# Order of transposes, logits, clearing and gate transfers at the entries of two expert blocks

## What is computed

```
x = conv attention (L0), then channel attention (L1)
t = tokens of x
t = t + L2_attn(layernorm(t))        # attention over the 8 images, per position
t = t + L2_ffn(layernorm(t))         # 8 experts, hidden 512, gelu, top 2 of softmax gates
t = t + L3_attn(layernorm(t))        # attention over the 256 positions, per image
t = t + L3_ffn(layernorm(t))         # 8 experts, hidden 256, silu(x w1) * (x w3), top 2, renormalised
```

```
logits = x @ gate_w + gate_b ; w = softmax(logits) ; keep the two largest, others 0
h = gelu(x @ w1[e] + b1[e])          # L3: silu(x @ w1[e]) * (x @ w3[e])
out = sum over e of gate[e] * (h @ w2[e] + b2[e])
```

## Time and profile before

| | us |
|---|---|
| median of 3 runs | 662.9 |
| lowest, highest | 662.83, 667.42 |
| profiled execution, its own time | 668.46 |
| its span in the profile | 666.7 |
| busy PE, DVE, ACT, POOL | 612.5, 535.1, 400.6, 146.0 |
| first expert block (layer 0) | starts at 152.6 |
| second expert block (layer 1) | starts at 505.2, to the end |

### The profile page before, as it was taken

The page is one execution under the profiler, slowest core; times in us unless marked ns, Lnnn a source line. Parts: engine busy times, 40 slices in busy tenths (PEclk is TensorE's granted clock), DMA queues, the critical chain, the costliest instruction groups (busy, mean ns, idle before and its releaser), DMA issues. The chain is left out here.

```text
span 666.7 us, 10013 instructions
## 1 busy us (share of the span) xinstructions
PE 612.5 (92%) x3186; PEld 483.1 (72%) x3186; DVE 535.1 (80%) x1153; ACT 400.6 (60%) x792; POOL 146.0 (22%) x117
## 2 busy tenths in 40 slices
PE   9998959997989999999997889999868889999996
PEld 5785458695768888887886777777746678888784
DVE  2736679967678778878788799999996699999986
ACT  4613221002958888888884799999873455555552
POOL 1193366645211101111011121111103011111200
PEclk9697587997889999999999555555556999999998
DMA  5000000002212220222000000000001242222200
GB/s 181 1 0 1 0 1 1 0 1 65 89 73 95 97 75 21 95 95 63 1 1 0 1 2 0 0 0 0 1 2 48 73 163 74 99 79 92 72 33 31
DMA packets 9699, 28.78 MB, mean 43 GB/s; under 512 B 960, under 2 KB 3264, under 8 KB 9536
## 3 DMA queue, kind: packets, MB, share of 16 engines
q1 hardware_dynamic: 9664, 28.34, 12.3%
HBM read 27.15 MB, written 1.18 MB: 43 GB/s over the span
## 5 line engine op out<-in xcount | busy, mean ns | idle before, releaser
L1327 DVE TENSOR_TENSOR hL<-hraw,hH 128x1024 fp32r<-128x1024 f32 (+1 forms) x128 | 131.4, 1053 | 35.2 <-ACT hH L1063 34.5
L1143 PE MATMUL ps<-xH,wH 128*128 128x512 f32 x256 | 103.5, 404 | 4.2 <-DVE hraw L1257 3.6
L1067 ACT ACTIVATE hraw<-ps,bias 128x512 f32<-128x512 f32 x128 | 86.8, 687 | 31.1 <-PE ps L1145 26.7
L1144 PE MATMUL ps<-xL,wH 128*128 128x512 f32 x256 | 102.7, 401 | 0.0
L1145 PE MATMUL ps<-xH,wL 128*128 128x512 f32 x256 | 102.6, 401 | 0.0
L996 POOL TENSOR_TENSOR wL<-wraw,wH 128x1024 fp32r<-128x1024 f32 (+1 forms) x16 | 35.6, 2227 | 236.1 <-DVE wH L1194 236.1
L1155 PE MATMUL ps<-hH,wH 128*128 128x512 f32 x192 | 77.2, 402 | 7.9 <-DVE hL L1327 7.9
L1157 PE MATMUL ps<-hH,wL 128*128 128x512 f32 x192 | 76.5, 398 | 0.0
L1156 PE MATMUL ps<-hL,wH 128*128 128x512 f32 x192 | 76.4, 398 | 0.0
L1063 ACT ACTIVATE hH<-hraw 128x1024 fp32r<-128x1024 f32 x64 | 67.5, 1055 | 1.0
L1072 ACT ACTIVATE hraw<-ps 128x512 f32<-128x512 f32 x64 | 38.3, 600 | 49.4 <-PE ps L1145 47.8
(11 more groups left out here) (247 smaller groups left out, 1197.3 us busy)
## 6 DMA issues: line engine op xcount, KB each, us to landing
G<-gates_scratch SPq DMA_DIRECT2D x32, 512.0 KB, 4.7
wraw<-in_ex SPq DMA_DIRECT2D x8, 514.5 KB, 5.7
wraw<-in_ex SPq DMA_DIRECT2D x8, 384.0 KB, 5.0
w<-in_pack SPq DMA_DIRECT2D x1, 1420.5 KB, 7.8
xs<-in_x SPq DMA_DIRECT2D x4, 256.0 KB, 4.6
out<-acc SPq DMA_DIRECT2D x4, 256.0 KB, 2.1
w<-in_pack SPq DMA_DIRECT2D x1, 501.0 KB, 3.7
gates_scratch<-gT SPq DMA_DIRECT2D x4, 32.0 KB
```

Of the source, the lines that this page charges most:

```text
L1067: act.activation(hraw[:, k % 2, h, :], ps[:, h, :], ACT.Gelu, bias=bias[:, place(k, last)[0], h:h + 1]).then_inc(z["act"], 1)
L1143: pe.matmul(o, wH[:, p, at:at + P], xa, start=True, stop=False)
L1144: pe.matmul(o, wH[:, p, at:at + P], xb, start=False, stop=False)
L1327: dve.tensor_tensor(hL[:, k % 2, g * half:(g + 1) * half, :], src, hi.bitcast(F32), ALU.subtract).then_inc(z["hl"], 1)
```

## The change

Numbered by place:

1. In `block2`, POOL clears acc behind the last normalisation scale of that block, once DVE has normalised the first half. In the entry of layer 0 only cmp is cleared, and not before DVE has normalised the second half.
2. In the entry of layer 0 the second half of the tokens is transposed with a signal after four columns and after eight, ACT copies it in two parts, and the logits follow each part. The filler before these logits is gone (the two fillers behind the first half's logits stay).
3. In layer 1 the logits of pair 0 come before the transposes of pair 1, the others behind the transposes of pair 3, and the filler is gone.
4. The residual transposes of pair 2 move from the end of the attention block into the entry of layer 1, those of pair 3 behind the transposed gates, into bank 6. The transposed gates wait for three copies of acc instead of four, and DVE's wait for acc moves in front of its first addition.
5. The first gate transfer is cut: the first 512 tokens of expert 0 are a transfer of their own with a semaphore of its own (`g0`), on which DVE's first gating waits. The second gating waits for the rest of the first half.

```diff
@@ block2, gpsimd
             ln_pool(pool, 1, 0)
+            pool.wait_ge(ln["nrm"], S + 1)
+            pool.memset(acc[:], 0.0).then_inc(s_rot, 1)
@@ experts, sync
                     for a_half in range(2):
                         c = slice(a_half * T // 2, (a_half + 1) * T // 2)
-                        sp.dma_start(G[:, p, c], gd[layer][bass.ds(e, 1), c].to_broadcast([P, T // 2])).then_inc(zw[p][1 + a_half], 16)
+                        if isinstance(j, int) and e == 0 and a_half == 0:
+                            sp.dma_start(G[:, 0, 0:CH], gd[layer][0:1, 0:CH].to_broadcast([P, CH])).then_inc(z["g0"], 16)
+                            c = slice(CH, T // 2)
+                        sp.dma_start(G[:, p, c], gd[layer][bass.ds(e, 1), c].to_broadcast([P, c.stop - c.start])).then_inc(zw[p][1 + a_half], 16)
@@ experts, gpsimd
                 if layer == 0:
                     ln_pool(pool, nn, 1)
-                chp.done(pool.memset(cmp[:], 0.0))
-                if layer == 0:
-                    pool.memset(acc[:], 0.0).then_inc(s_rot, 1)
+                    pool.wait_ge(ln["nrm"], S * nn + 2)
+                    pool.memset(cmp[:], 0.0).then_inc(s_rot, 1)
                 else:
+                    chp.done(pool.memset(cmp[:], 0.0))
                     pair_pool(pool, 3, c4)
@@ experts, scalar
                 if layer == 0:
-                    act.wait_ge(gs["ltp"], 2)
-                    act.activation(lnT[:, 1, :], flat(ps[:, 2:4, :]), ACT.Copy).then_inc(gs["lt"], 1)
+                    for g in range(2):
+                        act.wait_ge(gs["ltp"], 2 + g)
+                        act.activation(lnT[:, 1, g * CH:(g + 1) * CH], ps[:, 2 + g, :], ACT.Copy).then_inc(gs["lt"], 1)
                 else:
                     for c in range(NCH):
-                        if c == 2:
-                            tokens_out(act, 3, 7)
+                        if c == 1:
+                            tokens_out(act, 2, 7)
...
                         act.activation(gT[:], ps[:, 7, 0:P], ACT.Copy).then_inc(gs["gT"], 1)
+                        if layer == 1:
+                            tokens_out(act, 3, 6)
@@ experts, tensor
                     for s in range(S):
-                        pe.wait_ge(gs["lt"], s + 1)
-                        if s == 1:
-                            keep_busy(pe, 5, 1)
                         for b in range(B):
+                            if b % 4 == 0:
+                                pe.wait_ge(gs["lt"], s + 1 + s * (b // 4))
                             x = logits(s * B + b, lnT[:, s, b * P:(b + 1) * P])
                         if s == 0:
                             keep_busy(pe, 5, 2)
-                            ln_transposes(pe, nn, gs["ltp"], 1)
+                            ln_transposes(pe, nn, gs["ltp"], 1, 0, 4)
...
-                        pe.wait_ge(c4["acc"], NCH)
+                        pe.wait_ge(c4["acc"], 3)
...
                         gates_transposed()
+                        if layer == 1:
+                            tokens_transposed(pe, 3, 6)
@@ experts, vector
-                    dve.wait_ge(gs["lt"], s + 1)
+                    dve.wait_ge(gs["lt"], 1 + 2 * s)
...
-                    if c % 2 == 0:
+                    if isinstance(j, int) and item == 0:
+                        dve.wait_ge(z["g0"], 16)
+                    elif c % 2 == 0 or (isinstance(j, int) and item == 1):
                         dve.wait_ge(zw[p][1 + c // 2], 16 * (j + 1))
...
+                    if isinstance(j, int) and item == 0:
+                        dve.wait_ge(s_rot if layer == 0 else c4["acc"], 2 if layer == 0 else NCH)
...
-                dve.wait_ge(s_rot if layer == 0 else c4["acc"], 2 if layer == 0 else NCH)
@@ block4, scalar
-            for c in range(3):
+            for c in range(2):
                 tokens_out(act, c, SB + c)
@@ block4, tensor
-            tokens_transposed(pe, 2, SB + 2)
```

More of the change, by code:

```diff
@@ L941, in rounds @@
                     yield E // 2 - 1, k, True
-            z = {n: sem(f"ex{layer}_" + n) for n in "split wH hp act hm hH hl yp yg acc".split()}
+            z = {n: sem(f"ex{layer}_" + n) for n in "split wH hp act hm hH hl yp yg acc g0".split()}
             zw = [[sem(f"ex{layer}_{n}{p}") for n in ("w", "ga", "gb")] for p in range(2)]
-            fin = {n: sem(f"fin{layer}_" + n) for n in "tp done st".split()}
+            fin = {n: sem(f"fin{layer}_" + n) for n in ("tp done" if layer == 0 else "st").split()}
             nn = 1 + layer
@@ L1101, in _, with pair_logits @@
                             keep_busy(pe, 5, 2)
-                            ln_transposes(pe, nn, gs["ltp"], 1)
+                            ln_transposes(pe, nn, gs["ltp"], 1, 0, 4)
                 else:
-                    pair_transposes(pe, 0, c4)
-                    pair_transposes(pe, 1, c4)
-                    tokens_transposed(pe, 3, 7)
-                    keep_busy(pe, 4, 1)
-                    pair_transposes(pe, 2, c4)
-                    pair_transposes(pe, 3, c4)
-                    for c in range(NCH):
+                    def pair_logits(c):
                         pe.wait_ge(c4["lt"], c + 1)
@@ L1113, in _ @@
                             x = logits(i % 2 * B + 2 * c + i // 2, pair_columns(c)[:, i * P:(i + 1) * P])
+                        return x
+                    pair_transposes(pe, 0, c4)
+                    tokens_transposed(pe, 2, 7)
+                    pair_logits(0)
+                    for c in range(1, NCH):
+                        pair_transposes(pe, c, c4)
+                    for c in range(1, NCH):
+                        x = pair_logits(c)
                 x.then_inc(gs["lgp"], 1)
@@ L1241, in _ @@
                 if layer == 0:
-                    dve.wait_ge(s_rot, 2)
+                    dve.wait_ge(s_rot, 3)
                 for i in range(E):
```

## The result

| | before | changed |
|---|---|---|
| median of 20 runs each, side by side | 667.12 (661.27 to 670.88) | 660.77 (658.61 to 666.19) |
| ratio, 95% interval | | 0.9927 [0.9907, 0.9948] |
| own time and span of the profiled execution | 668.46, 666.7 | 661.98, 660.2 |

The change makes the kernel faster by 0.73%. The predicted 656.7 us is 4.1 us too low, and the median lies 0.27 us above the top of the range. The move itself was forecast nearly right: 656.7/662.9 is 0.9906, just under the interval above. Five executions of over 820 us, two of the kernel before and three of edited ones, are left out of every median here.

What follows compares the result with a forecast made beforehand. PE was taken as bound, busy in both expert blocks behind their entries, so microseconds won at entries stay won. 2.6+1.0+1.03-0.2+1.0 = 5.4, plus 0.8 for the clock, 6.2 off 662.9: 656.7 us, range 652.5 to 660.5.

Steps and rivals of the forecast that it cites:

- Against the median I take 5.4+0.8 = 6.2, so 656.7 us: Whole kernel: summed gains of 5.4 us plus 0.8 for half clock, taken from the three-run median of 662.9 us.
- The chain of entry one: Entry of the first expert block: DVE's gate chain starts at 163.2 instead of 165.86, a gain of 2.6 us.
- The clearing's move: Entry one: acc's clearing (1.9 us) costs nothing in the attention block; the eight xc end 1.73 us earlier.
- The chunk: Gate transfer in both entries: first gating waits for 256 KB less, a gain of 1.0 us each, between 0 and 2.6.
- The half clock behind the gate wait: Entry one, behind PE's wait for hL: no clock fall, 1.7 us in the profiled execution, 0.8 counted against the median.
- The block's end: End of the attention block: without the third token transpose and ACT's copy, DVE's add is last, a gain of 1.03 us.
- Entry two, -0.2: Second expert block's entry: new order with logits at half clock loses 0.2 us, between a 0.6 loss and 2.6 gain.
- The token pair behind the gates: Entry two, token pair 3 transposed while PE waits for hL: hidden, costing 0, at most 0.3 us.
- A: Rival, chance 0.20: entry two's logits at full clock (2.4 us more), entry one's cast early (0.6): 653.7 us.
- B: Rival, chance 0.17: the gate chunk lands no earlier; both 1.0 gains and the clock's 0.8 go: 659.5 us.
- C: Rival, chance 0.08: POOL holds entry one, wL is late, the chain gains 1.5 instead of 2.6 us: 657.8 us.
- D: Rival, chance 0.04: without fillers PE stays at half clock through each block's first 36 matmuls; slower, 665.7 us.

## Why the prediction was wrong

**The step that failed** is "Against the median I take 5.4+0.8 = 6.2, so 656.7 us". Its 6.2 is near what was measured: medians of 667.12 and 660.77 are 6.35 apart, the means of those runs 4.95 (665.97 and 661.02), the interval of the ratio allows 3.5 to 6.2, and the two repeats give 6.8 and 7.4 between medians. What failed is the time that it is taken from, the median of three runs: two of three lay near 662.9, where this kernel's median is 667. From 667.1 the same sum gives 660.9. The profiled execution, 5.6 us over that median, was the warning; I set 1.7 us of it down to a dip that the others might lack and left the rest open. The remark that below 1% a measurement can't tell this change from none was wrong too: 0.73% stands clear of it, with 20 runs of each.

**The chain of entry one, 2.6.** lg moved by 2.4 us and the ups by 2.0, with the forecast's mechanism (the cast ends with wL) and another cause for wL's time: the weights' landing, not the clearing. What passed through was G's issue, 24.77 to 22.08, so 2.7; on the means of three profiles it is 3.2. It follows the ups, not lg: the gates' transposition stands behind 24 ups on PE, and they take 7.1 to 8.5 us by the clock. That "PE's clock in the first 24 matmuls matters less" was wrong, and the right size of the term came out by luck: the ups moved less than expected and ran through faster (8.4 to 7.7).

**The clearing's move.** That its 1.9 us "cost nothing" held. Its benefit, which the chain counts with 1.73 us on the xc, was nothing where the weights landed late and up to 0.8 us for wL where they landed early: the sum had no term for the landing.

**The chunk, 1.0 per entry.** On the means of three profiles, 4.25 to 3.26 us in entry one and 4.30 to 3.26 in entry two: 1.0 each, as worked out from the rate. The estimate of 0.6 that followed from the Trainium skill ("DMA: Bandwidth & Descriptors", section "Anatomy of one DMA — SWDGE (gpsimd) path") is too little on this queue. That all landing rows here are longer than its rule gives is not so: out's 256 KB took 2.1 us, less than the 2.6 that one would estimate by that rule.

**The half clock behind the gate wait, 1.7.** In entry one no profile with the change has it, but of three of before only the first did (177.6 us from G's issue to the last gating against 175.5 and 175.9), so counting half of it was somewhat too much. In entry two, for which the sum has no such term, the changed kernel's second profile and those of nine edited kernels fell to 1.2 GHz for 3.4 us behind waits of 1.9 to 2.7 us, while five others, with waits of 1.85 to 2.1, did not. The length of the last wait alone doesn't decide it. The kernel before kept its clock in entry two behind a longer wait than any of these:

```profile
535.30 0.50 PE L1143 MATMUL ps<-xH,wH 128*128 128x512 f32 x1 [2.90 <-DVE hraw L1257]
```

In its third profile it fell at 528.4 (0.50 in the window from 528.5 to 531.5), behind a wait of only 1.21 us that ended at 527.4, where the prediction expects no fall. In the changed kernel the stretch from the first gating to the end takes 132.8 us without and 134.8 with the fall. This price of 2 us is paid in some executions and not in others. What decides it stays open.

**The block's end, 1.03.** From DVE's last add to the block each pair of profiles gives 1.01, the means between the blocks 1.3; undoing it alone costs 0.5 there, with the transposes at full clock.

**Entry two, -0.2.** The twelve logits took 0.43 each, as forecast, in two of three profiles, but the ups came 10.82 us after the start and not 11.2, against 11.6 before; in the third profile logits ran at 0.24 and the ups came at 8.92 (the best of before: 10.44). That is 0.8 to 1.5 us gained where I had a loss. The means to the first gating agree: 2.4 us, of which the chunk is 1.0. In the table this is the term furthest off, 1.6 us. (The working also gives the tokens 0.8 us and four logits 1.5 at prices of 1.06 and 4 x 0.43, which is 0.5 too little.) The token pair behind the gates was hidden, as said: with it back in its old place PE's wait behind the gate transfer is 1.90 us, with the change 1.96.

**Rivals.** A's clock came in some executions, at entry two. B is out by the landing rows. C's mechanism is what the changed profiles show, xL and with it PE held by wL, but at 2.0 us gained by the ups and not 1.5, and wL was late for the weights. D is out: the kernel became faster, and either filler put back leaves the time the same.

## What to carry to other kernels

Take the time before from many runs, or forecast the ratio and apply it to whatever median the comparison will have: three runs of a kernel that spreads over 10 us can be 4 us off, more than most terms of such a sum. When a chain is shortened, follow it through every engine on which its next link is queued: the gates were ready earlier, but their transposition stood behind 24 matmuls, and behind each removed wait another, for DVE or POOL, came next. Before moving an instruction out of another's way, look whether the victim would have waited for something else, here in some executions for the weights' transfer.

## What the runs showed of the hardware

Which DVE instructions POOL's subtraction blocks depends on their operands. Those that read and write SBUF alone wait for its end (cast 2.57 instead of 0.69 us, hL 2.53 instead of 1.28, addition 1.82 instead of 0.69), while xL from PSUM takes 1.23 beside wL when ACT has made xH, and 1.23 alone. The Trainium skill ("SBUF — State Buffer", section "SBUF: two separate sides") names two-port modes and two SBUF inputs as what takes the shared ports; the rows agree. In the kernel with the product moved ahead, whose entry one is unedited, the weights came so late that the cast slipped in front of wL:

```profile
162.94 0.69 DVE L1217 CAST xH<-lnT 128x1024 fp32r<-128x1024 f32 x1
163.02 2.83 POOL L1001 TENSOR_TENSOR wL<-wraw,wH 128x1024 fp32r<-128x1024 f32 x1 [1.80 <-DVE wH L1207]
```

The cast took 0.69 us and wL 2.83 instead of 2.35, and lg came 8.9 us after the block's start instead of 10.8. The first weights landed 4.6 to 6.3 us after the start in the 18 profiled executions, here latest of all. So the landing of a transfer can decide a matter of 2 us for DVE, though the ups then wait for wL (10.0).

The granted clock of the same instructions at the same place differs from one execution to the next (twelve logits in 5.13 or 2.93 us, a fall behind the second gate wait in some). That this makes much of the kernel's spread fits its runs, in which the time falls as the mean granted clock rises, from 0.832 with 667.7 to 671.0 us to 0.849 with 662.3.
